# Four exchanges in a fused attention and expert kernel: engine order, weight-tile placement, attention matmul shape, bias matmul rows

## The reference

```
x = x + cross_attention(layernorm(x), ctx)    # x: 8 x 64 x 512, ctx: 8 x 1601 x 512, 16 heads of 32,
                                              # weights max(s,0)+1/(1+max(-s,0)), divided by their sum
x = x + self_attention(layernorm(x))          # 8 query heads of 64, one key/value head, causal softmax
x = x + ffn(layernorm(x))                     # mean of 2 shared experts + top 2 of 8 routed experts
                                              # expert: gelu(x W1 + b1) W2 + b2, hidden size 2048
```

## Time and profile before

| | |
|---|---|
| time, median of 3 runs | 1297.12 us (1295.58 to 1297.34) |
| profiled execution, own time | 1297.12 us |
| its span, first to last instruction | 1295.3 us |
| granted TensorE clock, mean | 0.998 |
| busy: PE, PEld, DVE, ACT, POOL | 99%, 87%, 49%, 48%, 31% |
| HBM traffic | 133 GB/s over the span |

### The profile page before, as it was taken

One profiled execution on the slowest core, in us unless ns is written; L12 is line 12 of the kernel. 1 busy time (PEld: TensorE's weight loads), 2 busy tenths in 40 slices (PEclk: granted clock), 3 DMA queues, 4 the chain that ended last, 5 costly groups with the idle time before them and its releaser, 6 DMA issues.

```text
span 1295.3 us, 31424 instructions
## 1 busy us (share of the span) xinstructions
PE 1280.3 (99%) x13820; PEld 1126.9 (87%) x13820; DVE 639.8 (49%) x971; ACT 623.9 (48%) x1093; POOL 405.4 (31%) x212
## 2 busy tenths in 40 slices
PE   8999999999999999999999999999999999999997
PEld 6898898888888889888889889798989998999896
DVE  5334443544543543453443444666776555565654
ACT  4444554544445444644543546547534444554443
POOL 1344344444454443445445444200032000100000
PEclk9999999999999999999999999999999999999999
DMA  6131111121111102121112121564566499999990
GB/s 221 62 107 34 35 39 34 34 70 63 38 65 33 49 22 99 35 79 34 35 38 100 58 91 63 229 259 163 171 184 211 152 335 362 345 340 343 372 366 34
DMA packets 34941, 174.98 MB, mean 135 GB/s; under 512 B 6184, under 2 KB 8392, under 8 KB 18544
## 3 DMA queue, kind: packets, MB, share of 16 engines
q1 hardware_dynamic: 33056, 168.16, 36.3%
q0 software_dynamic: 1744, 4.76, 1.1%
HBM read 166.84 MB, written 6.06 MB: 133 GB/s over the span
## 4 chain that ended last, share of the span: by engine, by line
PE 95%; DVE 2%; ACT 1%; issue 1%; DMA 1%; PEldq 0%; SPq 0%; DVEq 0%; PEld 0%; ACTq 0%
PE bank L691 23%; PE bank L703 22%; PE bank L1016 11%; PE sc L1033 9%; PE sc L719 8%; PE sc L879 6%; PE bank L732 4%; PE bank L898 3%; PE sc L898 3%; PE bank L791 1%; PE bank L755 1%; PE bank L839 1%; DMA xres<-in_x 1%; PE bank L854 1%; PE sc L854 1%
## 5 line engine op out<-in xcount | busy, mean ns | idle before, releaser
L557 POOL TENSOR_TENSOR xn<-xn,tt 128x1024 f32<-128x1024 f32 x96 | 231.2, 2408 | 364.6 <-DVE tt L1247 364.4
L1133 ACT ACTIVATE tt<-sc 128x512 f32<-128x512 f32 (+1 forms) x208 | 107.8, 603 | 393.2 <-PE sc L719 393.2
L1338 DVE TENSOR_TENSOR wsl<-ring,wsh 128x2048 fp32r<-128x2048 f32 x72 | 167.7, 2330 | 113.8 <-ACT wsh L1093 110.9
L691 PE MATMUL bank<-cxh,wkh 128*128 128x256 f32 (+1 forms) x752 | 222.4, 296 | 1.0 <-DVE va L1242 1.0
L691 PE MATMUL bank<-cxl,wkh 128*128 128x256 f32 (+1 forms) x752 | 215.9, 287 | 0.5 <-issue 0.5
L691 PE MATMUL bank<-cxh,wkl 128*128 128x256 f32 (+1 forms) x752 | 215.1, 286 | 0.0
L1234 DVE TENSOR_SCALAR kk<-bank,bkt 128x256 f32<-128x256 f32 (+1 forms) x190 | 93.3, 491 | 202.1 <-PE bank L691 202.1
L703 PE MATMUL bank<-wvh,cxh 128*128 128x512 f32 (+1 forms) x416 | 165.1, 397 | 0.0
L703 PE MATMUL bank<-wvl,cxh 128*128 128x512 f32 (+1 forms) x416 | 164.5, 395 | 0.0
L703 PE MATMUL bank<-wvh,cxl 128*128 128x512 f32 (+1 forms) x416 | 163.5, 393 | 0.0
L1093 ACT CAST wsh<-ring 128x2048 fp32r<-128x2048 f32 x72 | 137.3, 1907 | 45.5 <-PE sc L1033 21.2
(11 more groups left out here) (257 smaller groups left out, 1966.0 us busy)
## 6 DMA issues: line engine op xcount, KB each, us to landing
ring<-in_w SPq DMA_DIRECT2D x112, 1024.0 KB, 7.0
ctxt<-in_ctx SPq DMA_DIRECT2D x40, 512.0 KB, 3.7
ctxt<-in_ctx SPq DMA_DIRECT2D x8, 642.0 KB, 4.0
wqt<-in_wo SPq DMA_DIRECT2D x4, 1024.0 KB, 6.5
wqt<-in_aq SPq DMA_DIRECT2D x4, 1024.0 KB, 7.1
wqt<-in_ap_ SPq DMA_DIRECT2D x4, 1024.0 KB, 5.7
yrows<-K SPq DMA_DIRECT2D x1, 2048.0 KB, 9.9
tt<-in_wk SPq DMA_DIRECT2D x2, 512.0 KB, 5.4
```

The source lines that it names most:

```text
L557: e.tensor_tensor(dacc[0:kn, y, :], dacc[0:kn, y, :], tt[0:kn, w, :], ALU.add).then_inc(s["da_pool"], 1)
L691: m = e.matmul(dst[:, 0:n], (wkh, wkl)[a][:, c, g * P:(g + 1) * P], (cxh, cxl)[b][:, u, c, 0:n], start=(c == 0 and x_ == 0), stop=(c == 3 ...
L1338: e.tensor_tensor(wsl[m % 3][:], ring[slot(unit_split(m))][:], wsh[m % 3][:].bitcast(F32), ALU.subtract).then_inc(s["wl_dve"], 1)
```

## The change

Six edits are made together. (1) DVE does the weights of a group's second chunk at the end of the group's own slot, after the late keys, instead of in the next slot ahead of the early keys. (2) `normalised` does its first half three slots after the end of a batch entry and its second half four slots after it. (3) The buffers of split weights 1 and of ring 3 and 4 change places in memory: `weights_hi(1)` waits for the last values and moves with `weights_split(1)` to slot NCH-1, `weights_hi(2)` loses its wait, and ring 3 and 4 are loaded after the last keys. (4) `attended` is one matmul with 128 columns of weights and 512 moving columns, and DVE takes the two wanted halves out with two copies. (5) The expert weights are turned by four transposes into 10 partitions x 512 columns, and the four bias matmuls all read those 10 partitions. (6) b2 is loaded once instead of four times.

```diff
-            if last:
-                nrm.append((b, 0, 4))
+            nrm.append((b, 0, 4 if last else 2))
         if lag == 4 and not last:
-            nrm += [(b, 0, 2), (b, 2, 2)]
+            nrm.append((b, 2, 2))
...
-        b2t = sb("b2t", [P, D])
+        b2t = sb("b2t", [10, D])
...
-        wts = sb("wts", [P, 4, 32])
+        wts = sb("wts", [P, 4, 10])
...
-        wT = pT[:, 0:P]
+        wT = pT[0:10, :]
...
+        early_ring = [sb(f"ring{i}", [P, 2048]) for i in range(3, 5)]
         wsh1, wsl1 = sb("wsh1", [P, 2048], F32R), sb("wsl1", [P, 2048], F32R)
-        early_ring = [sb(f"ring{i}", [P, 2048]) for i in range(3, 5)]
...
-            for t in range(4):
-                e.dma_start(b2t[32 * t:32 * t + 10, :], b2).then_inc(s["small_in"], 16)
...
-            e.wait_ge(s["v_pe"], NCH)
+            e.wait_ge(s["k_pe"], 4 * NPART)
             for n in range(3, 5):
                 load_shared(n)
...
-                pv = pT.rearrange("p (h x t) -> p x h t", h=4, x=2)
-                for x_ in range(2):
-                    m = e.matmul(dst[64 * x_:64 * x_ + 64, 0:256], V2[r, 0:64], pv[r, x_, :, :], start=True, stop=True)
-                m.then_inc(s["o_pe"], 1)
+                e.matmul(dst[:], V2[r, :], pT[r, :], start=True, stop=True).then_inc(s["o_pe"], 1)
...
-                    m = e.matmul(bank[1][32 * t:32 * t + 32, 0:P], wts[:, t, :], ident[:], start=True, stop=True)
+                    m = e.transpose(bank[1][0:10, 128 * t:128 * t + 128], wts[:, t, :], ident[:])
...
-                    r = slice(32 * t, 32 * t + 10)
-                    m = e.matmul(bank[4 + t][:], wT[r, :], b2t[r, :], start=False, stop=True, skip_group_check=True)
+                    m = e.matmul(bank[4 + t][:], wT[:, P * t:P * t + P], b2t[:], start=False, stop=True,
+                                 skip_group_check=True)
...
                 if m == 1:
-                    e.wait_ge(s["k_pe"], 4 * NPART)
-                elif m == 2:
                     e.wait_ge(s["v_pe"], NCH)
...
-                if n == NCH - 2:
+                if n == NCH - 1:
                     weights_hi(1)
...
-                src = pj[use["o", t, b] % 2][:, 0:256].rearrange("p (h t) -> p h t", h=4)
-                e.tensor_copy(ov[:, :, b, :], src).then_inc(s["proj_read"], 1)
+                src = pj[use["o", t, b] % 2][:].rearrange("p (h x t) -> p h x t", h=4, x=2)
+                for x_ in range(2):
+                    q = slice(64 * x_, 64 * x_ + 64)
+                    m = e.tensor_copy(ov[q, :, b, :], src[q, :, x_, :])
+                m.then_inc(s["proj_read"], 1)
...
-                for m in group(n - 1)[1:]:
-                    weights(m, 0)
-                    weights(m, 1)
                 for i, g in early:
                     keys(i, g)
                 for m in group(n)[:1]:
                     weights(m, 0)
                     weights(m, 1)
                 for i, g in late:
                     keys(i, g)
+                for m in group(n)[1:]:
+                    weights(m, 0)
+                    weights(m, 1)
...
-                if n == NCH - 2:
+                if n == NCH - 1:
                     weights_split(1)
```

More of the change, by code:

```diff
@@ L395, in sync @@
             for dst, src in ((bqt[:], bq), (bvt[:], bv), (bot[:], bo), (bpt[:], abp), (rbt[:], rb), (rwt[:], rw),
-                             (b1s[:, 0, :], b1[8]), (b1s[:, 1, :], b1[9]), (akt[:], ak), (avt[:], av)):
+                             (b1s[:, 0, :], b1[8]), (b1s[:, 1, :], b1[9]), (b2t[:], b2), (akt[:], ak), (avt[:], av)):
                 e.dma_start(dst, src).then_inc(s["small_in"], 16)
-            for t in range(4):
-                e.dma_start(b2t[32 * t:32 * t + 10, :], b2).then_inc(s["small_in"], 16)
             def store_rows(t):
@@ L797, in self_keys @@
                 if t == 0:
-                    e.wait_ge(s["small_in"], 224)
+                    e.wait_ge(s["small_in"], 176)
                 for c in range(4):
@@ L1174, in act @@
                     e.wait_ge(s["wt_pe"], 1)
-                    e.copy(wT, bank[1][:, 0:P]).then_inc(s["wT_act"], 1)
+                    e.copy(wT, bank[1][0:10, :]).then_inc(s["wT_act"], 1)
             e.wait_ge(s["rt_dve"], RT_INT)
```

## The result

The changed kernel took 1326.77 us (median of 4 runs) against 1296.48 before: ratio 1.0236 with a 95% interval of 1.0216 to 1.0256, so it is slower by 30 us. I had forecast 1307.8, with 1312 as the upper end. The direction was right, the size a third of the true one. The executions of the kernel before fall into two groups, near 1295.4 and near 1297.0 us, 1.6 us apart, which is about what one stretch of half clock costs, and the profiled one, from which the sum was built, is of the upper group.

What follows compares the result with a forecast made beforehand. PE, busy 1280.3 of 1295.3 us, was taken as the bound. Terms 2.2 + 1.65 + 2.7 + 1.45 + 0.3 + 2.35 + 0.1 = 10.75 on 1297.1 gave 1307.8 us, range 1302 to 1312.

Steps and rivals of the forecast that it cites:

- Half of the division, earlier: Attention, two slots after an entry's start: value copy late, new 0.67 us PE wait for four entries, +2.7 us.
- weights of the second chunk, earlier: Attention, slots opening a batch entry: value copy slips, three 0.35 us PE waits grow by 0.55 each, +1.65 us.
- the distance of two reciprocals, 1.65: DVE in slot 28: cost of half a division, read from reciprocals at 247.68 and 249.33, placed ahead of the value copy.
- the subtraction at 812.98: End of attention: subtraction took 1.8 us over its mean beside a POOL sum; 0.5 us of overlap charged in the new place.
- the three entries that I had put at 0.05: Batch entries 2, 4 and 6: the slot holds attended, PE is later, so the earlier half division adds at most 0.05 us.
- 0 elsewhere: Other attention slots: earlier second-chunk weights delay the copy by 0.1 to 0.5 us, harmless with 0.7 spare, so 0.
- The clock: End of attention: half clock follows PE's idleness; 1.7 us charged again behind the new 4.6 us wait.
- Split weights 1: End of attention: old gap's 4.1 us go, a 4.6 us wait plus 1.7 us of half clock come, +2.2 us.
- Biases: Expert bias matmuls: four in one row group run serially, 3.43 us instead of 1.08, +2.35 us.
- The full factor of four: Rival at the bias matmuls: tiling's full factor makes serial time 4.3 us, sum 0.9 higher, 1308.7 us; chance 0.03.
- attended: Tiles in attention: two matmuls run together, about 0.95 us a tile, +1.45; DVE's four copies add 0.3 us.
- four rivals: No effect inside attention 1303.4 (0.17); serial attended, longer low clock 1311.3 (0.10); not slower 1296.2 (0.08); full factor 1308.7 (0.03).

Runs made afterwards that it cites:

- product in PSUM: Kernel before plus earlier second-chunk weights and earlier half division, the division writing its product to PSUM, where the bias add reads it: 1305.62 us, ratio 1.0072.
- the run alone: Kernel before plus only b2 loaded once, expert weights turned by transposes and four serial bias matmuls on the same 10 rows: 1300.73 us, ratio 1.0030.
- the half division first: Kernel before plus earlier second-chunk weights and earlier half division, the half division ahead of those weights within the slot: 1307.6 us, ratio 1.0084.
- the biases spread: Kernel before plus b2 once, transposes and serial bias matmuls, one bias matmul in each of four successive slots: 1299.62 us, ratio 1.0024.

## Why the prediction was wrong

The losses of the parts alone, taken from the ratios, are 1.62% (edits 1 and 2), 0.22% (3), 0.22% (4) and 0.30% (5 and 6): 2.36%, the whole. Taken together their intervals leave some 0.3% open, about 4 us; a larger further part there isn't.

- *Half of the division, earlier* (+2.7 forecast) and *weights of the second chunk, earlier* (+1.65) are the failed step. Together they cost 21 us. I costed the half division at "the distance of two reciprocals, 1.65", as if that distance were its own, and took it to another place in the slot. What went with it is the bias add, whose time depends on what POOL does beside it. In the row that I used, the add already stood for 0.14 us at the end of a POOL sum, 0.43 where the other half takes 0.29. This is its timeline in the kernel before:

```profile
248.98 0.43 DVE L1371 TENSOR_TENSOR xT<-xT,bvt 128x128 f32<-128x128 f32 x1
250.63 0.29 DVE L1371 TENSOR_TENSOR xT<-xT,bvt 128x128 f32<-128x128 f32 x1
```

In the new place it meets POOL's subtraction with 1.3 us or more of it to go. I had priced just such an overlap for the subtraction at 812.98 and not asked it of the adds. The waits were 1.8 us instead of 0.67, and the three entries that I had put at 0.05 had 1.5. The run with the product in PSUM, with waits of 0.62, shows that the rest of that step was right. Edit 2 is free alone, edit 1 costs 4 us: the price is in the pair. The "0 elsewhere" of edit 1 was too low as well, by 2 to 3 us: its three large waits came as said (0.95 us each), and ten smaller waits of weight loads that the sum hadn't.

- The Trainium skill has this under "SBUF — State Buffer", Who interferes with whom: a DVE instruction with two SBUF inputs contends with a GpSimd instruction that reads SBUF, one with at most one such input outside the 2-port modes doesn't. Both halves agree with the traces of this add: 1.50 us against 0.29, beside the same subtraction of POOL. Applied to L1371 in its new place, it would have had the add end with POOL's instruction, in all seven slots; measured, that is 1.2 us more in four and 1.5 to 1.7 in three.
- *The clock*: I charged it at the old gap's place only. New stretches came behind some of the long waits (at most 1.7 us each) and one in the bias matmuls; over the whole kernel 17 us more at half clock, some 8 us of time. I had concluded that the clock "follows PE's idleness"; at the biases it fell with PE busy throughout. Half clock isn't certain after a wait: the 2.1 us wait has it in the kernel before, not in the runs with edits 1 and 2.
- *Split weights 1* (+2.2): mechanism, place and the 4.6 us right; the clock's share was 2.4 us, 0.3 over its upper bound.
- *Biases* (+2.35): serial, as said, but 3.6 to 4.3 us with half clock behind them, 3.9 us alone. The full factor of four that the Trainium skill allows ("TensorEngine Tiling (Array Packing)", Theoretical Speedup) would have made them 4.3; at full clock they took 3.63, a factor of 3.4, so it was not what made the difference.
- *attended* (+1.75): together, as said; 1.11 us instead of 0.95, and 2.9 us by the ratio.
- The chances: three of the four rivals were on the cheaper side or next to the forecast, and none let two edits meet. The range followed them.

## What to carry to other kernels

When an instruction is moved, ask not only who stands behind it in its queue but what the other engines do at the time to which it goes, and whether that work shares a way into memory with it and with the instructions that it pushes back. A price read from a row holds for the neighbours that it had there. A long instruction that must run beside POOL belongs where the queue has nothing urgent behind it: a place between a copy that PE waits for and weights that wait for ACT gave 0.2%.

## What the runs showed of the hardware

- A DVE add of 128 x 128 fp32 with both inputs in SBUF takes 0.29 us. Started beside a POOL subtraction (edits 1 and 2), it took 1.50 to 1.99 us and ended 0.14 to 0.16 us after it, seven times of seven; with one input in PSUM it took 0.29 beside the same subtraction, seven times of seven.
- Two inputs in SBUF aren't the only form that stands: L1347, a `tensor_scalar` of 128 x 512 from SBUF to SBUF, took 1.28 and 1.49 us where it was begun while POOL's subtraction L579 ran (subtraction of split weights 1 in slot NCH-1 and in slot NCH), and 0.42 to 0.43 in the kernel before.
- The granted clock fell to 0.50 in the middle of, or right behind, four serial matmuls with 10 rows, though PE was busy throughout (993 in the changed kernel, 967 in the run alone), and it did not when the same matmuls stood between full ones.
- The wait of 2.1 us ahead of the last weighted sums was followed by a fall in five traces (before, edit 1, edit 2, edit 4, edits 5 and 6) and not in four (edits 1 and 2, the half division first, the product in PSUM, the biases spread); of the four waits of 1.8 us in the changed kernel, two were.
- Two fp32 matmuls of 64 rows x 128 columns x 512 in different row halves ran side by side in 1.11 us, four of 10 rows in different row groups in 1.08.
